# Cross-attention values with the softmax weights stationary, in float16 parts, and one ring of PSUM banks

## What is computed

```python
x = x + self_attention(layernorm(x))                       # 16 heads of 16, causal, ALiBi
q, k, v = ln(x) @ Wq + bq, ctx @ Wk + bk, ctx @ Wv + bv      # 16 heads of 64
attn = softmax(q @ k.T / 8)                                # per head, 2048 x 1601
out = (attn @ v) @ Wo + bo + ln(x)
x = x + (layernorm(out) * gamma + beta)
x = x + (fp8_gemm(layernorm(x)) + bias)                    # 256 x 256
```

## Time and profile before

| | us |
|---|---|
| median of the three executions | 2211.42 |
| the profiled execution, its own time | 2230.43 |
| span in its trace | 2228.5 |
| PE busy in the span | 1964.8 |
| DVE, ACT, POOL busy | 1247.4, 879.5, 1027.2 |

### The profile page before, as it was taken

How to read it: one execution, slowest core, us unless ns; L and a number is a source line. 1 busy time by engine, 2 the same in 40 slices (tenths; PEclk the granted TensorE clock), 3 DMA queues, 4 the chain that set the end, 5 groups by cost and what they waited for, 6 DMA issues and landing times.

```text
span 2228.5 us, 32080 instructions
## 1 busy us (share of the span) xinstructions
PE 1964.8 (88%) x11994; PEld 1069.0 (48%) x11994; DVE 1247.4 (56%) x2495; ACT 879.5 (39%) x1762; POOL 1027.2 (46%) x856
## 2 busy tenths in 40 slices
PE   6888998899988998899999999899899899989762
PEld 3544444444444554455555555555555555545331
DVE  4666677765613646645535635644554654653668
ACT  2234566655654222233333433343343343334331
POOL 1000000000002445547767766766776776769774
PEclk9667999987978898999999999999999999999885
DMA  5222211240010000000000000000000000000001
GB/s 103 26 31 30 30 16 17 31 92 1 11 38 29 8 1 8 1 1 10 1 1 11 1 1 11 1 1 10 1 1 3 1 1 3 1 26 3 1 19 38
DMA packets 27746, 34.63 MB, mean 16 GB/s; under 512 B 3986, under 2 KB 25811, under 8 KB 25939
## 3 DMA queue, kind: packets, MB, share of 16 engines
q1 hardware_dynamic: 27592, 32.59, 8.2%
HBM read 14.99 MB, written 4.19 MB: 9 GB/s over the span
## 4 chain that ended last, share of the span: by engine, by line
PE 75%; DVE 11%; issue 6%; ACT 4%; POOL 2%; SPq 1%; DMA 1%; POOLq 0%; DVEq 0%; ACTq 0%
PE psum L857 17%; PE psum L842 12%; DVE maxima L1107 7%; PE psum L830 7%; PE psum L750 7%; PE psum L664 5%; PE psum L725 5%; PE psum L698 4%; PE psum L846 4%; ACT weights_room L943 3%; PE psum L880 3%; PE psum L818 2%; PE psum L868 2%; PE psum L762 2%; PE psum L734 1%
## 5 line engine op out<-in xcount | busy, mean ns | idle before, releaser
L1107 DVE TENSOR_REDUCE maxima<-psum 128x1 f32<-128x400 f32 (+5 forms) x1664 | 882.4, 583 | 456.9 <-PE psum L830 276.9
L1348 POOL TENSOR_TENSOR parts_room<-parts_room,weights_room 128x512 f32<-128x512 f32 (+1 forms) x596 | 746.8, 1286 | 339.1 <-ACT weights_room L1001 339.0
L1001 ACT ACTIVATE weights_room<-psum 128x512 f32<-128x512 f32 (+1 forms) x694 | 370.0, 597 | 610.6 <-PE psum L846 608.7
L943 ACT ACTIVATE weights_room<-psum 128x512 f32<-128x512 f32 (+3 forms) x640 | 298.0, 535 | 253.6 <-PE psum L725 136.5
L1310 POOL TENSOR_SCALAR rstd<-meanvar 128x2 f32<-128x2 f32 (+1 forms) x24 | 6.7, 280 | 701.9 <-DVE meanvar L1057 701.9
L842 PE MATMUL psum<-stack_room,k_hi 64*128 64x512 f32 (+1 forms) x1664 | 304.0, 411 | 9.3 <-ACT weights_room L1001 7.7
L830 PE MATMUL psum<-k_hi,stack_room 64*128 64x400 f32 (+1 forms) x1024 | 254.3, 404 | 37.0 <-DVE maxima L1107 34.8
L830 PEld LDWEIGHTS psum<-k_hi,stack_room 64*128 64x128 f32 x1024 | 145.5, 189 | 215.3 <-issue 124.3
L725 PE MATMUL psum<-stack_room,stack_room 51*128 51x512 f32 (+3 forms) x640 | 203.7, 458 | 41.1 <-ACT weights_room L943 39.9
L842 PEld LDWEIGHTS psum<-stack_room,k_hi 64*128 64x128 f32 (+1 forms) x1664 | 167.8, 185 | 59.6 <-issue 29.2
L846 PE MATMUL psum<-shifts,parts_room 64*128 64x512 f32 (+1 forms) x832 | 189.8, 395 | 0.0
(11 more groups left out here) (119 smaller groups left out, 1798.4 us busy)
## 6 DMA issues: line engine op xcount, KB each, us to landing
stack_room<-parts_room SPq DMA_DIRECT2D x96, 128.0 KB
x_block<-x_dram SPq DMA_DIRECT2D x8, 512.0 KB, 4.7
x_middle<-x_block SPq DMA_DIRECT2D x4, 512.0 KB, 3.1
x_block<-x_middle SPq DMA_DIRECT2D x4, 512.0 KB, 5.4
out_dram<-x_block SPq DMA_DIRECT2D x8, 256.0 KB, 2.1
parts_room<-ctx_dram SPq DMA_DIRECT2D x1, 1536.0 KB
stack_room<-shift_rows SPq DMA_DIRECT2D x64, 2.0 KB
parts_room<-wq_dram SPq DMA_DIRECT2D x8, 128.0 KB, 2.3
```

The costliest lines, as they stand in the source:

```text
L943: engine.activation(w_self[s % NW][:, m, 0:n], self_scores[(HP * s + m) % SELF_SCORES][:, 0:n], ACT.Exp, scale=SELF_SCALE).then_inc(exp_do ...
L1001: engine.activation(weights[u % NP_WEIGHTS][:kw, :], pair_scores[u % NSCORES][:kw, :], ACT.Exp, scale=CROSS_SCALE).then_inc(pair_exp, 1)
L1107: engine.tensor_reduce(maxima[:, p % 2, i // TB, n, i % TB, ch:ch + 1], bank_of(use + n)[:, 0:real - k0], AX.X, ALU.max) \
L1348: engine.tensor_tensor(sum_[:kw, m, :], old[:kw, :], new, ALU.add).then_inc(weights_added, 1)
```

## The change

- The values product is turned round. The weights (128 keys x 128 queries) are stationary and v streams, 64 columns and a column of ones, so the sum over the keys comes out as column 65 and queries are on the partitions. The weights are kept as two float16 parts (high, low), v too. For each head and step there are 4 x 3 matmuls: high times [v high, 1], high times v low, low times [v high, 1]. The two heads accumulate in a bank each.
- ACT makes the exponential twice from the same scores: float32 (`w_whole`, 5 buffers) and float16 (`w_hi`, 10 buffers), both with a bias of 8 ln 2 read from SBUF. The low part is their difference, made on POOL, and for the second head on DVE where j is 1, 5 or 9, and in all of pair 7. The score banks are free after the second exponential.
- v is scaled for each pair by a power of two: maxima on DVE (`value_top`), over the partitions on POOL (`partition_all_reduce`, `value_all`), the scale on DVE (`value_scale`), the high part on ACT, the low part on DVE (`value_parts`).
- The sums on POOL, `pair_sums` and the copy of the products go. DVE divides (`pair_finish`), PE turns the block (`pair_turn`), ACT copies it, and `pair_project` multiplies both heads at once, in two banks.
- Scores, chunks and all others share one ring of 6 banks.
- The value tiles of pair 0 come before its queries instead of beside its first block.

```diff
-SUMS_LAG, PROJECT_LAG = 4, 4
+PAIR_TURN_LAG, PROJECT_LAG = 2, 2
-CROSS_RING, NSCORES = 3, 4
-NW, NP_WEIGHTS = 5, 12
+CROSS_RING = 6
+NW, NWHOLE, NPART = 5, 5, 10
+V_BITS, WEIGHT_BITS = 13, 8
...
-            self.put("pair_scores", p, b, j, self.step)
+            self.put("pair_scores", p, b, j, self.step, banks=HP)
...
-        self.put("pair_project", p, b, banks=4)
+        self.put("pair_project", p, b, banks=2)
...
+    def with_split(self, p, steps):
+        steps = list(steps)
+        for n, kind in enumerate(("value_all", "value_scale", "value_parts")):
+            steps.insert(3 * n + 2, (0, lambda kind=kind: self.put(kind, p)))
+        return steps
...
+    def on_vector(p, b, j, m):
+        return m == HP - 1 and (p == NP - 1 or j % 4 == 1)
...
+                slots = [take_bank(use + m) for m in range(HP)]
...
-                        if n == 0 and u >= NSCORES:
-                            pe.wait_ge(pair_exp, u - NSCORES + 1)
...
-                    engine.matmul(products[r:r + DH2, :], v_pair[p % 2][:kw, j, r:r + DH2],
-                                  weights[u % NP_WEIGHTS][:kw, :], start=j == 0, stop=j == NS - 1) \
-                        .then_inc(pair_values_done, 1)
+                    hi = w_hi[(HP * s + m) % NPART]
+                    pe.wait_ge(*bank_read(scores_use + m))
+                    for t in range(TB):
+                        engine.matmul(pair_products[:, m, t, :], hi[:kw, t * P:(t + 1) * P], v[:kw, j, m, 0:V_WIDE],
+                                      start=j == 0 and t == 0, stop=False, skip_group_check=True)
+                        engine.matmul(pair_products[:, m, t, 0:DH2], hi[:kw, t * P:(t + 1) * P],
+                                      v[:kw, j, m, V_WIDE:V_WIDE + DH2], start=False, stop=False,
+                                      skip_group_check=True)
+                for m in range(HP):
+                    lo = w_lo[(HP * s + m) % NPART]
+                    pe.wait_ge(*lo_made[HP * s + m])
+                    for t in range(TB):
+                        last = engine.matmul(pair_products[:, m, t, :], lo[:kw, t * P:(t + 1) * P],
+                                             v[:kw, j, m, 0:V_WIDE], start=False, stop=j == NS - 1,
+                                             skip_group_check=True)
...
-                    engine.activation(weights[u % NP_WEIGHTS][:kw, :], pair_scores[u % NSCORES][:kw, :], ACT.Exp,
-                                      scale=CROSS_SCALE).then_inc(pair_exp, 1)
+                    if u >= NWHOLE:
+                        act.wait_ge(*lo_made[u - NWHOLE])
+                    engine.activation(w_whole[u % NWHOLE][:kw, :], bank_of(use + m)[:kw, :], ACT.Exp,
+                                      bias=weight_bits[:kw, :], scale=CROSS_SCALE).then_inc(whole_made, 1)
...
+                    engine.activation(w_hi[u % NPART][:kw, :], bank_of(use + m)[:kw, :], ACT.Exp,
+                                      bias=weight_bits[:kw, :], scale=CROSS_SCALE).then_inc(emptied(use + m), 1)
...
+                    if on_vector(p, b, j, m):
+                        dve.wait_ge(*bank_read(use + m))
...
+                        engine.tensor_tensor(w_lo[u % NPART][:kw, :], w_whole[u % NWHOLE][:kw, :],
+                                             w_hi[u % NPART][:kw, :], ALU.subtract).then_inc(lo_on_vector, 1)
...
+                engine.partition_all_reduce(v_top[:, 1:2], v_top[:, 0:1], P, bass.bass_isa.ReduceOp.max) \
+                    .then_inc(v_top_all, 1)
```

263 lines of the change are left out of this document (149 added, 114 removed).

## The result

Four executions of the changed kernel have a median of 2405.7 us (2389.9 to 2420.1), the kernel before in the same session 2220.4: a ratio of 1.084, 95% interval [1.074, 1.094]. The forecast was 2350 us with a range up to 2470 and slower as its sign. The time is inside the range and the sign is right. The sum behind it is right partly by luck: its largest term had a part of the wrong sign, other terms were too small, and pair 0 and pair 7 missed in opposite directions.

What follows compares the result with a forecast made beforehand. PE was taken to have nearly no slack. Middle blocks +142 us, pair 0 -15, pair 7 0 and scaling of v +14 gave +141 on 2211.4: 2352, say 2350; own range 2280 to 2420, 8 in 10 2210 to 2470.

Steps and rivals of the forecast that it cites:

- Values on PE: Values product: 24 matmuls a step at 0.040 us, 0.96 us where there were 0.94; by itself no gain.
- Rival B: Values product: small matmuls 0.060 us apart or more, +6.2 us a block, 2500 us in all; chance 0.12.
- The ring, and ACT twice: Middle blocks: doubled exponentials hold shared banks longer, a three-chunk batch takes 5.9 us instead of 4.46; +6.3 us a block.
- The bias: ACT's exponentials: reading bias from SBUF, 688 instead of 598 ns; spacing 0.49 to 0.58 us, taken as 0.575.
- Sums, turn, projection: Middle blocks: sums leave PE, -1.85 us; the turn adds 0.45; projection waits for DVE go, -1.1.
- Low parts on DVE: Middle blocks: three low parts behind ACT's last exponential delay chunk maxima and next chunks; +2.1 us a block.
- Scaling of v: Once a pair, 8 times: maxima, low part and POOL's all-reduce taken as 4 us, 1.7 lost each; +14 us.
- rival C: POOL's all-reduce is long: 9 us each gives 2390 us, with code loads about 2440; sign over 5 us; chance 0.14.
- Pair 0: First pair: six banks instead of three give chunks room, some 3.75 us a block less; -15 us, bounds -35 and +20.
- Pair 7: Last pair, without chunks: POOL, then ACT and copies set its pace; change 0, bounds -25 and +25 us.
- The clock: PE's clock in middle blocks, a sign in the changed trace: perhaps below the 0.97 of now.
- Rival A: The ring does not bind and PE's relief counts: -1.4 us a block, -35 in all, 2176 us; chance 0.15.

Runs made afterwards that it cites:

- e11: Changed kernel with low parts of pairs 0 to 6 on POOL, banks released early, bias folded into shift rows, maximum by DMA: 2136.8 us, 0.948 of before.
- e10: Kernel before with one ring of 6 banks for scores, chunks and other uses instead of 4 and 3: 2124.6 us, 0.954 of before.
- e9: Kernel before with one ring of 7 banks and every cross-attention exponential taken twice, without bias: 2167.1 us, 0.975 of before.
- e4: Changed kernel with exponentials lacking their bias operand, so weights are not scaled by 2^8: 2342.4 us, 1.055 of before.
- e3: Changed kernel with all low parts of pairs 0 to 6 made on POOL, none on DVE: 2336.6 us, 1.052 of before.
- e2: Changed kernel without the all-reduce, the scale of v taken for each partition by itself: 2369.6 us, 1.071 of before.
- e6: Kernel before with one ring of 7 banks for scores, chunks and other uses instead of 4 and 3: 2064.2 us, 0.936 of before.
- e12: Changed kernel with its 6 banks cut into two rings, 3 for scores and 3 for all else: 2660.9 us, 1.197 of before.
- e7: Changed kernel with banks released after the float32 exponential and low parts of the first seven pairs on POOL: 2174.5 us, 0.980 of before.
- e1: Changed kernel with banks released after the first exponential, the float16 part copied from its SBUF tile: 2426.5 us, 1.098 of before.

## Why the prediction was right, and where it was wrong

- **Values on PE.** Forecast 0.040 us a matmul, measured 0.031 at full clock: 0.75 us a step where it was 0.94, which would be 13 x 0.19 = 2.5 us a block that I had put at nothing. In the changed kernel 0.7 of it arrives (table by stage), since the matmuls there take 0.040 in the mean, clock and waits included; that this is the forecast's number is chance. In e11 it is 2.6. Rival B (0.060) is out. The Trainium skill, "TensorE: Matmul & The Clock Gate", section "Back-to-back issue gap", gives its 81 ns for 128 columns; these runs show 31 ns at 65, so the figure doesn't carry over to them.
- **The ring, and ACT twice: +6.3 a block. A part of this step had the wrong sign.** It treated the ring as a cost only. It reads the batch of 5.40 us as one with a fourth chunk. It has three, like the one of 4.46, and the 0.94 between them is what the ring of 3 costs. PE's waits for DVE were there to see: 21.7 us before chunks and 26.3 before projections, and 17.1 more before projections that the reading left out. The runs put the ring of 6 at -2.5 a block (e10), of which 1.3 is in the projections, and the second exponential in a ring of 7 at +4.5 (e9, without bias). With 2.3 for the bias (e4), which the forecast's 0.575 included, that makes -1.2 + 4.5 + 2.3 = +5.6. So by its parts the term is near its forecast. This is an estimate from three different kernels, since ring of 6 and second exponential together were not run. The coupling that the step describes is real.
- **The bias** was inside the 0.575 and not priced by itself. The spacing was right (0.575), and it costs 2.3 us a block (e4). A block has 52 exponentials, and 52 x 0.083 = 4.3 us, so about half of what ACT saves reaches the block.
- **Sums, turn, projection: -1.85 + 0.45 - 1.1 = -2.5.** By stage -1.1 for sums and turn, since the turn takes 0.8 us and not 0.45, and -1.6 for the projections, whose waits were 43.4 us and not 26.3.
- **Low parts on DVE: +2.1 a block.** Mechanism right, size somewhat too small: 2.9 (e3). DVE waits for ACT, the maxima wait behind, and the scores wait for these.
- **Scaling of v: +14 us.** Too small: 29 to 36 (e2), nearer the +40 of rival C. By the prediction's own sign, POOL standing for over 5 us at each all-reduce, rival C was right. POOL's pause of 5.8 us before the all-reduce is what the Trainium skill, "GPSIMD Engine Reference", section "Instruction dispatch", says of loading code (about 6); the trace agrees, and shows a second pause of 6.7 behind it. So the pauses were as long as rival C's page had it, 12.5 us, and the loss only some 4 us a pair; that POOL's slack elsewhere takes up the rest is argued, not shown.
- **Pair 0: -15, measured +24.** With a ring of 6 in the kernel before pair 0 took 158.9 us between its first and last mark (787.13 to 946.06), and 176.7 before, -17.8; the second exponential adds 7.1 in a ring of 7 (159.2 in e9, 152.1 in e6). That is -11, where the forecast for both was -15. What failed is that low parts, bias and scaling were charged to the 24 middle blocks alone or hardly at all. In the changed kernel the same stretch is 200.8 us; without DVE's low parts 185.5 (e3), without the bias 190.4 (e4), without the all-reduce 195.5 (e2), with all four edits 157.3 (e11). The first three are worth 15.3, 10.4 and 5.3, and -11 with these is +20 of the +24.
- **Pair 7: 0, measured -18.** Nearly all of it lies after the last mark (37.8 instead of 53.8 us to the end of the span). One ring in the kernel before gives 49.2 to 49.9 there (e6, e10), and every kernel with the new product has 37.7 or 37.8, with 3 + 3 banks too (e12), so the ring is not the main part. The marks are not the same event in the two kernels, and the rest stays open.
- **The clock** was foretold as "perhaps below 0.97" and given no term. In the middle blocks it was 0.90 in the changed kernel, 0.93 in e3, 0.97 in e11 and 1.00 in e6: broadly it falls as PE's idle time grows (187, 169, 81 and 6 us), but not strictly, since e2 has 157 us and 0.90. A wait removed can thus be worth more than its length.
- **Rival A** had the right idea, that PE's relief counts once nothing binds. e11 shows it after four edits, but most of its 3.2 us a block is the ring's gain (2.5 in e10), which A did not foresee either.

In a middle block the forecast, with the scaling of v, was 42.9 + 6.5 = 49.4, and 50.1 came. By parts: product -0.7, sums and turn -1.1, projections -1.6, ring and exponentials with their bias +5.6, low parts +2.9, all-reduce +1.4: +6.5, and +7.2 was measured. The sum closes better than it deserves. The parts are taken out of different kernels, and they don't simply add: release and low parts together gave 8.1 a block (e7) where alone they gave -0.9 and 2.9. Pair 0 (39 too low) and pair 7 (18 too high) cancel in part as well.

## What to carry to other kernels

Before you price the coupling of a shared ring, price the coupling that the divided ring already has. Here PE's waits for DVE were 65 of 1030 us in the middle blocks, one ring of 7 took them all away, and nearly as much again came out of PE's busy time. When two batches differ in length, count what each holds before you call the difference work: the two of the earlier trace rows hold the same three chunks. One small edit tests it. When a stall has two engines in series (ACT frees late, DVE reads late), taking away one can show nothing (e1), and that is no proof that it costs nothing (e7): remove the other too before you drop it. And put no instruction that waits for a late producer ahead of the short ones that free banks.

## What the hardware showed that I had not expected

- Float16 matmuls with a new stationary operand for each 64 or 65 streaming columns go 0.031 us apart at full clock, 24 in 0.75 us, and 24 x 2 in a batch without a break (1508.79 to 1510.37).
- The all-reduce leaves POOL idle on both sides, 5.82 and 6.71 us around 0.38 us of work: going back to plain instructions costs at least as much as going there.
- GpSimd's subtraction with a float16 output and one float16 operand takes 1161 ns, the addition of the same shape in float32 1278. Operation and type differ together, so neither is shown to be the reason.
- DVE's low part, one shape in one kernel family, has a mean of 741 ns in the changed kernel, 956 in e4 and 1212 in e1. What differs is how long it runs beside POOL's own low parts. In the middle blocks of the changed kernel all 72 last about 692 ns, with some 45 ns of it beside POOL; in e1 they last 1.27 us, with 0.72 us beside POOL. One of e1, POOL's row and then DVE's:

```profile
1499.35 3.39 POOL L1427 TENSOR_TENSOR weights_room<-parts_room,weights_room 128x512 f16<-128x512 f32 x3 [1.81 <-ACT weights_room L1051]
1502.01 1.27 DVE L1256 TENSOR_TENSOR weights_room<-parts_room,weights_room 128x512 f16<-128x512 f32 x1 [3.94 <-ACT weights_room L1051]
```

Here DVE starts 0.73 us before POOL's row ends (1502.74) and ends 0.54 us after it. In the changed kernel the low part of 1532.12, shown above, starts 0.04 us before the end of POOL's row (1528.70 to 1532.16) and takes 0.69. DVE's low part is longer by most of the time that it stands beside POOL's.
